# The second block one chunk behind the first, its mixing ahead of the first group means, and the adapter's weights later

## What is computed

```
L0 cond:  y = einsum('bct,bcd->bdt', x, w[subject])           # mixes the 64 tokens of a sample
L0 ffn:   gu = y @ Wq_gu^T ; h = silu(gate) * up ; hn = rms_norm(h) ; x = x + hn @ Wq_p^T
          Wq = ternary quantisation of W in groups of 64 (scale = mean |w| of the group)
L1 cond:  H = x @ W^T + (x @ A[idx]^T) @ B[idx]^T * s[idx]    # a low-rank adapter per sample
L1 ffn:   router logits, softmax over 8 experts, the best 2, weighted sum of expert outputs ; x = x + that
```

## Time and profile before

| | |
|---|---|
| runs, median (lowest to highest) | 2326.0 us (2324.54 to 2328.16) |
| the profiled execution | 2326.22 us |
| its span in the trace | 2324.5 us |
| TensorE busy | 2296.1 us, 99% |
| VectorE busy | 1669.5 us, 72% |
| ScalarE busy | 1146.7 us, 49% |
| mean granted clock of TensorE | 0.998 |

### The profile page before, as it was taken

One profiled execution on the slowest core, in us unless ns is written; L12 is line 12 of the kernel. 1 busy time (PEld: TensorE's weight loads), 2 busy tenths in 40 slices (PEclk: granted clock), 3 DMA queues, 4 the chain that ended last, 5 costly groups with the idle time before them and its releaser, 6 DMA issues.

```text
span 2324.5 us, 30032 instructions
## 1 busy us (share of the span) xinstructions
PE 2296.1 (99%) x10288; PEld 1893.4 (81%) x10288; DVE 1669.5 (72%) x2497; ACT 1146.7 (49%) x1685; POOL 11.2 (0%) x20
## 2 busy tenths in 40 slices
PE   7999999999999998999999999999999999999999
PEld 5777888888888887888888888888888888888887
DVE  8985434334343435888899999998988888888883
ACT  7754333333232324788888888888522222222221
POOL 0000000000000000000000000000000000000000
PEclk9999999999999999999999999999999999999999
DMA  5314202111111115121111112114422222222220
GB/s 200 109 41 138 75 19 74 37 56 56 54 38 54 72 36 199 59 82 62 56 68 68 68 59 81 54 63 162 173 91 72 90 93 70 89 94 70 89 81 23
DMA packets 103332, 184.66 MB, mean 79 GB/s; under 512 B 12210, under 2 KB 45554, under 8 KB 100978
## 3 DMA queue, kind: packets, MB, share of 16 engines
q1 hardware_dynamic: 51554, 124.77, 15.3%
q10 hardware_dynamic: 51600, 59.25, 7.7%
q0 software_dynamic: 128, 0.07, 0.0%
HBM read 122.72 MB, written 61.34 MB: 79 GB/s over the span
## 4 chain that ended last, share of the span: by engine, by line
PE 91%; issue 5%; DVE 2%; ACT 1%; DMA 1%; ACTq 0%; POOLq 0%; POOL 0%; SPq 0%; DVEq 0%
PE slot L1501 17%; PE ex L1672 10%; PE ex L1673 10%; PE ex L1674 10%; PE plane L1633 10%; PE plane L1635 10%; PE plane L1637 10%; PE pj L1514 8%; PE slot L1554 3%; PE slot L1476 1%; PE slot L1543 1%; PE slot L1533 1%; DVE ew_lo L1386 0%; PE slot L1486 0%; DMA q_raw<-in_w_ffn 0%
## 5 line engine op out<-in xcount | busy, mean ns | idle before, releaser
L1501 PE MATMUL slot<-y_hi,wgu 128*128 128x512 f32 x1024 | 403.1, 394 | 2.2 <-DVE q_scale L1052 1.7
L1501 PE MATMUL slot<-y_lo,wgu 128*128 128x512 f32 x1024 | 399.1, 390 | 0.0
L1633 PE MATMUL plane<-rw_hi,hb 128*128 128x512 f32 x1008 | 393.3, 390 | 1.7 <-ACT plane L855 0.9
L1635 PE MATMUL plane<-rw_hi,hb 128*128 128x512 f32 x1008 | 393.1, 390 | 0.0
L1637 PE MATMUL plane<-rw_lo,hb 128*128 128x512 f32 x1008 | 392.9, 390 | 0.0
L1672 PE MATMUL ex<-ew_hi,hb 128*128 128x512 f32 x992 | 386.0, 389 | 0.2 <-ACT ex L983 0.2
L1673 PE MATMUL ex<-ew_hi,hb 128*128 128x512 f32 x992 | 385.9, 389 | 0.0
L1674 PE MATMUL ex<-ew_lo,hb 128*128 128x512 f32 x992 | 385.9, 389 | 0.0
L983 ACT ACTIVATE ex<-eb_sb 128x512 f32<-128x512 f32 x248 | 149.0, 602 | 449.2 <-DVE acc L1415 386.1
L1361 DVE SCALAR_TENSOR_TENSOR lead_in<-code_in,wts 128x1024 bf16<-128x1024 bf16 x256 | 311.4, 1216 | 1.2
L1094 DVE TENSOR_TENSOR hid<-gate,slot 128x512 f32<-128x512 f32 x112 | 76.9, 687 | 221.7 <-ACT gate L690 221.1
(11 more groups left out here) (155 smaller groups left out, 3222.2 us busy)
## 6 DMA issues: line engine op xcount, KB each, us to landing
hb<-h_scratch SPq DMA_DIRECT2D x34, 512.0 KB, 3.3
h_scratch<-ht ACTq DMA_DIRECT2D x64, 256.0 KB, 3.1
code_scratch<-half_code SPq DMA_DIRECT2D x64, 256.0 KB, 2.0
half_in<-code_scratch SPq DMA_DIRECT2D x32, 512.0 KB, 3.3
hb<-h_scratch ACTq DMA_DIRECT2D x30, 512.0 KB, 3.6
q_raw<-in_w_ffn SPq DMA_DIRECT2D x21, 512.0 KB, 3.4
x_scratch<-x_res ACTq DMA_DIRECT2D x8, 1024.0 KB, 4.5
rraw<-in_rwT SPq DMA_DIRECT2D x8, 1024.0 KB, 10.9
```

The costliest lines, as they stand in the source:

```text
L1501: last = mm(slot[s % 2][:, g, :], wgu[:, c, r * P:(r + 1) * P], y[:, c, :], start=(c == 0 and v == 0), stop=(c == DC - 1 and v == 1))
L1633: mm(bank[:, :, :], hb[:, u, c, 0, :], rw_hi[:, w, c, o], start=False, stop=False, skip_group_check=True)
L1635: mm(bank[:, :, :], hb[:, u, c, 1, :], rw_hi[:, w, c, o], start=False, stop=False, skip_group_check=True)
```

## The change

Block 1 runs one chunk behind block 0 and not two (`AHEAD = 1`): pair h issues block 1's chunks 2h-1 and 2h, and only chunk 15 is left for after the loop. Block 1's mixing goes from behind gu(0,1) to directly behind gu(0,0), ahead of the two group means of that pair, on TensorE, ScalarE and VectorE. AT, Bt, the indices and the scalings are loaded behind `load_raw(8)` into buffers of their own (which share their place with the lo parts); `small_weights` goes from the end of the pair h = 0 to just ahead of `linear_weights`, on ScalarE and VectorE, and the product's wait for it is gone. Behind the loop, chunk 1's `second_hidden` comes ahead of the last silu and product of block 1. On TensorE the adapter product and the two linear products of block 0 each go one down product later.

```diff
-AHEAD = 2
+AHEAD = 1
...
     FIRST.append(f"gu{_j}@0")
     GU_ORDER.append((0, _j))
     if _h:
-        FIRST.append(f"gu{_j - 2}@1")
-        GU_ORDER.append((1, _j - 2))
-    FIRST += [f"q{k}" for k in quant_of(_h)[:2]]
-    FIRST.append(f"gu{_j + 1}@0")
-    GU_ORDER.append((0, _j + 1))
-    if _h:
         FIRST.append(f"gu{_j - 1}@1")
         GU_ORDER.append((1, _j - 1))
     else:
         FIRST += ["mix0@1", "mix1@1"]
+    FIRST += [f"q{k}" for k in quant_of(_h)[:2]]
+    FIRST.append(f"gu{_j + 1}@0")
+    GU_ORDER.append((0, _j + 1))
+    FIRST.append(f"gu{_j}@1")
+    GU_ORDER.append((1, _j))
     FIRST += [f"q{k}" for k in quant_of(_h)[2:]]
...
+        small_raw = ExitStack()
+        a_raw = sb("a_raw", [P, DC, P], F32, small_raw)
+        b_raw = sb("b_raw", [P, D], F32, small_raw)
+        small_raw.close()
         a_lo = sb("a_lo", [P, DC, P], F32R, pa)
+        b_lo = sb("b_lo", [P, D], F32R, pa)
         b_hi = sb("b_hi", [P, D], F32R, pa)
-        b_lo = sb("b_lo", [P, D], F32R, pa)
...
             gather_mix(1, mixw1, mixw1_in, range(3, SPB))
-            sp.dma_start(hid1[:, RING - 2, :].rearrange("p (c n) -> p c n", c=DC),
-                         AT.rearrange("(c p) n -> p c n", p=P)).then_inc(raw_small, 16)
-            sp.dma_start(hid1[:, RING - 1, :], Bt).then_inc(raw_small, 16)
-            sp.dma_start(idx_i[:, :], idx6).then_inc(small_in, 16)
-            sp.dma_start(scal_sb[:, :], scal).then_inc(small_in, 16)
             for k in range(5, NU):
                 load_raw(k)
+                if k == 8:
+                    sp.dma_start(a_raw[:, :, :], AT.rearrange("(c p) n -> p c n", p=P)).then_inc(raw_small, 16)
+                    sp.dma_start(b_raw[:, :], Bt).then_inc(raw_small, 16)
+                    sp.dma_start(idx_i[:, :], idx6).then_inc(small_in, 16)
+                    sp.dma_start(scal_sb[:, :], scal).then_inc(small_in, 16)
...
@@ ScalarE
                 silu(0, j)
                 quant_out(3 * h + 1)
                 if h:
-                    silu(1, j - 2)
+                    silu(1, j - 1)
+                else:
+                    mix(1)
                 quant_out(3 * h + 2)
...
                 high(0, j + 1, hid[:, (j + 1) % 2, :])
-                if h:
-                    silu(1, j - 1)
-                else:
-                    mix(1)
+                silu(1, j)
                 if h < PAIRS - 2:
                     quant_in(3 * h + 6)
-                if h == 0:
-                    small_weights()
             second_hidden(0)
-            silu(1, HC - 2)
-            for p in range(1, 4):
+            second_hidden(1)
+            silu(1, HC - 1)
+            for p in range(2, 4):
                 second_hidden(p)
-            silu(1, HC - 1)
             store_x1(0)
+            small_weights()
             linear_weights()
...
@@ VectorE
                 n, s = use(1, f"gu{j}")
                 dve.wait_ge(gate_ready, gu_count(1, j) + 1)
-                if j in (RING - 2, RING - 1):
-                    dve.wait_ge(w_lo_ready, 2)
...
                 product(0, j)
                 if h:
                     squares(0, j - 1)
-                    second_product(j - 2)
+                    second_product(j - 1)
+                else:
+                    mix(1)
...
                 low(0, j + 1, hid[:, (j + 1) % 2, :])
-                if h:
-                    second_product(j - 1)
-                else:
-                    mix(1)
+                second_product(j)
                 if more:
                     quant_sign(b)
-                if h == 0:
-                    small_weights()
             squares(0, HC - 1)
             finish(0)
             second_hidden(0)
-            second_product(HC - 2)
-            for p in range(1, 4):
+            second_hidden(1)
+            second_product(HC - 1)
+            for p in range(2, 4):
                 second_hidden(p)
-            second_product(HC - 1)
+            small_weights()
             linear_weights()
...
@@ TensorE
                 gu(0, j)
                 if h:
-                    gu(1, j - 2)
+                    gu(1, j - 1)
+                else:
+                    mix(1)
                 if more:
                     quant(3 * h + 3)
...
                 gu(0, j + 1)
-                if h:
-                    gu(1, j - 1)
-                else:
-                    mix(1)
+                gu(1, j)
                 proj(0, j)
...
-                if p == 4:
+                if p == 5:
                     adapt(0)
-                if p == 6:
+                if p == 7:
                     linear(0, 0)
-                if p == 9:
+                if p == 10:
                     linear(0, 1)
```

More of the change, by code:

```diff
@@ L156, in first_block @@
     return isinstance(i, int) and i == 0
-assert len(REST) % 2 == 0 and len(FIRST) % 2 == 0 and len(SECOND) % 2 == 0
+assert len(REST) % 2 == 0 and (len(FIRST) + len(SECOND)) % 2 == 0
 def build(nc, x, idx7, idx6, cond_w, w_ffn, WcT, AT, Bt, scal, rwT, rb, ewT, eb, out):
@@ L638, in small_weights @@
                 act.wait_ge(raw_small, 32)
-                nc.scalar.activation(a_hi[:, :, :], hid1[:, RING - 2, :].rearrange("p (c n) -> p c n", c=DC), ACT.Copy).then_inc(w_hi_ready, 1)
-                nc.scalar.activation(b_hi[:, :], hid1[:, RING - 1, :], ACT.Copy).then_inc(w_hi_ready, 1)
+                nc.scalar.activation(a_hi[:, :, :], a_raw[:, :, :], ACT.Copy).then_inc(w_hi_ready, 1)
+                nc.scalar.activation(b_hi[:, :], b_raw[:, :], ACT.Copy).then_inc(w_hi_ready, 1)
             def linear_weights():
@@ L1020, in small_weights @@
                 dve.wait_ge(w_hi_ready, 2)
-                nc.vector.tensor_tensor(a_lo[:, :, :], hid1[:, RING - 2, :].rearrange("p (c n) -> p c n", c=DC),
+                nc.vector.tensor_tensor(a_lo[:, :, :], a_raw[:, :, :],
                                         a_hi[:, :, :].bitcast(F32), ALU.subtract).then_inc(w_lo_ready, 1)
-                nc.vector.tensor_tensor(b_lo[:, :], hid1[:, RING - 1, :], b_hi[:, :].bitcast(F32), ALU.subtract).then_inc(w_lo_ready, 1)
+                nc.vector.tensor_tensor(b_lo[:, :], b_raw[:, :], b_hi[:, :].bitcast(F32), ALU.subtract).then_inc(w_lo_ready, 1)
                 dve.wait_ge(small_in, 32)
```

## The result

The changed kernel took 2328.46 us (median of 18 runs, 2327.57 to 2332.85), the kernel before 2324.59 us in the same session (18 runs, 2324.03 to 2328.45). The ratio is 1.0018, 95% interval 1.0011 to 1.0024: slower by about 4 us. The interval leaves out no change, and the difference is just under the 0.2% that the prediction called a difference. The profiled execution of the changed kernel has a span of 2329.0 us against 2324.5.

What follows compares the result with a forecast made beforehand. TensorE bounds the kernel, busy 2296.1 of 2324.5 us; only its idle can be won. 2326.22 - 2.4 + 2.5 + 0.9 = 2327.2, against the median 2326.0: 2327.0 us, range 2325 to 2330.

Steps and rivals of the forecast that it cites:

- Part 1: First pair, 23 to 50 us: TensorE reaches quant(7) 1.3 us later with 3.64 us more done, -2.4 us.
- part of the 2.4: First pair: small weights' removal takes 1.91 us off VectorE, counted within the 2.4 us gain, not separately.
- Part 2: Pairs 1 to 7: same step order and drains, cost 0; bounds 0 and 0.3 us for each pair.
- Rival C: Steady pairs no longer close, TensorE waits for quant(a)'s scale: 2 to 5 us more, 2329 to 2332; chance 0.10.
- Part 3: End of the opening, from row sums' end to adapter product: idle 4.4 us in place of 1.95, +2.5 us.
- the forecast's idle of 4.4: TensorE's idle between row sums' end and adapter product: 20.7 us less 16.3 us of work.
- only 0.65 of VectorE's 1.91 lasts: Small weights ahead of the linear weights: 1.25 of VectorE's 1.91 us goes into existing waits, 0.65 delays.
- Rival B: End doesn't bite: adapter product's input ready 20.07 us or less behind row sums' end; 2324 us, chance 0.21.
- Part 4: Behind the second linear product: only four down products follow, the last waits for its split, +0.9 us.
- T at about 175.1: Sign of being right: the row-sum matmuls end at about 175.1 us, against 177.46 before.
- rival E: TensorE falls to its low clock after longer idle; adapter product and two down products cost 5 us: 2332, chance 0.05.

Runs made afterwards that it cites:

- mix_early: Kernel before with only block 1's mixing moved directly behind gu(0,0), still two chunks apart, small weights where they were: median 2329.89 us.
- small_late: Kernel before with only the small weights in own buffers, loaded behind load 8 and split ahead of the linear weights: median 2324.04 us, ratio 0.9994.
- fill_end: Changed kernel with eight idle matmuls ahead of block 0's adapter product: median 2328.97 us.
- small_pair7: Changed kernel with small_weights moved to the end of pair 7 on ScalarE and VectorE: median 2327.42 us.
- fill_front: Changed kernel with eight idle matmuls in the first pair, six between quant(3) and quant(4), two behind quant(4): median 2328.59 us.
- after: The changed kernel itself, as first measured and profiled against the kernel before: median 2328.46 us, ratio 1.0018.
- after_again: The changed kernel measured once more, nothing edited: median 2330.26 us.
- lin_back: Changed kernel with block 0's second linear product back behind position 9 of the down products: median 2329.74 us.
- best: Kernel before plus small weights in own buffers, loaded late and split where engines are idle, and the adapter product behind down product 5: median 2320.95 us, ratio 0.9977.
- before_adapt5: Kernel before with only block 0's adapter product behind down product 5, not 4: mean 2324.3 us, ratio 0.9994.

## Why the prediction was right or wrong

It gave 2327.0 us and +1.0 us; measured were 2328.46 and +3.9 us. The time lies in the range and within 0.2%, where 0.84 of the chance stood. That it is only 1.5 us off is in part luck: the forecast started from a median of three, 2326.0, and the median of 18 is 1.4 us lower, so as a change it is 2.9 us off. The direction was right and the schedule nearly (+1.5 for +1.0). Of the rest of the miss, low clock in the opening, to which the sum gave nothing, is about 1.4 us in the means, and what is left is open. Part of the 3.9 is that the median of the kernel before falls among its executions at 0.999 and that of the changed kernel among those at 0.998. Of the executions at 0.998 the changed kernel's take 2328.1 us and those of the kernel before 2326.3: 1.8 apart, close to the schedule's 1.5.

**Part 1, the first pair: mechanism right, size off by 0.4.** The waits stand where it put them: quant(3) 0.38, quant(4) 1.62, gu(0,1) 0.52 us (forecast 0.35, 1.6, 0.7), and gu(1,0) runs directly behind. (One of quant(3)'s two matmuls is absent from that trace; where both are there, in `mix_early`, the wait is 0.16.) The forecast counts a little differently: from the release to gu(0,1) it has 5.31 us, and it is 5.55; the pair of products behind takes 7.55 at full clock and not 7.40. Without low clock release to T is 154.07 to 154.09, 1.65 longer than before with 3.64 more work: -2.0 us, not -2.4. With it, 1.65 us more are lost. The runs of single parts show what this net is made of, if the parts simply add up: the early mixing costs 2.16, the small weights' removal gives 1.89, and the rest, the second block one chunk behind, gives 1.65 - 2.16 + 1.89 = 1.38 longer with 3.64 us more done, so 2.3 us; it covers the down product's wait of 2.0 that the mixing opens. That the removal of the small weights was "part of the 2.4" was an understatement: it is nearly all of it.

**Part 2, the steady pairs: right.** From 50 to 170 us TensorE is busy 119.59 us in the changed kernel (120.00 before), and the list of waits names none there. The 0.41 are six group means of which the trace has one matmul only, starting 0.07 us after the step ahead of it ends; the step itself is no longer than the others. Rival C is out.

**Part 3: right in the sum, the reading of it too kind.** The adapter product came at T+20.71; forecast T+20.7. The first down product waits 1.0 us (forecast 1.1) and the adapter product 1.9; a second wait of 0.7 us, of down product 4 behind the small and the linear weights on VectorE, is in the forecast's idle of 4.4 but was not named. That only 0.65 of VectorE's 1.91 lasts held in the changed kernel (+0.64), but alone on the kernel before the same move costs 1.14. Rival B is out.

**Part 4: right.** 0.7 us of wait and a slower restart ahead of down product 14; undoing the move gave 1.0 us, forecast 0.9.

**The sum without low clock** is +1.5 between the same points (+1.54, +1.46 and +1.44 in three traces), against the forecast's +1.0; the missing half is part 1.

**A slip.** "T at about 175.1" contradicts the prediction's own sum: quant(7) 1.3 us later and no change in the steady pairs puts T at 178.8. Measured without low clock it is 178.63 from a release at 24.54, or 179.1 for the release at 25.04. A reader who had used that line to test the steps would have found a fault that isn't one.

**The clock, rival E, is where the forecast failed.** It put the clock at nothing in its sum and at 0.05 as a rival, by two waits ahead of the first products (4.33 us low, 2.15 us not). Neither carries that. The first pair of the same trace takes just as long:

```profile
5.42 1.01 PE L1486 MATMUL slot<-q_mag,group_mean 128*128 128x512 bf16 x2 [5.42 <-ACT q_mag L660]
```

So the pair behind 4.33 us of idle was no slower than the one before it, and a fall of the clock in between isn't shown. And behind the 2.15 us the clock was low in two other traces. What happened is a fall of the clock where several short waits stand near each other: 0.38, 1.62 and 0.52 us with a group mean between them, and 1.0, 0.7 and 1.9 us within 17 us, with down products between. No wait of these is as long as 2.15, and a single one of 2.9 in `small_late` was followed by no fall. So the length of the last wait doesn't decide it. Nor do short waits near each other by themselves: the same three in the first pair kept the clock at 1.00 in the traces of `fill_end` and `small_pair7`, and the same three at the adapter product did in `fill_front`. The price was too high: the low clock lasts about 3.4 us, not the adapter product and two down products, and costs 1.65 and 1.55 us, 3.2 together, not 5. Weighted with 13 of 29 executions this is 1.4 us of the mean, if 0.996 stands for both stretches. The Trainium skill (TensorE: Matmul & The Clock Gate, HAM oscillation) says that idle gaps between groups of matmuls can bring the clock down. The traces of the changed kernel agree, at 0.50 in both stretches. The next section of the same page of the Trainium skill (A second HAM failure mode: psum-queue depth-cycling) tells of a clock that swings because the engine idles briefly and often between groups of matmuls. That is nearer to this case than the long wait I weighed; when it happens it doesn't say, and some traces here kept their clock with the same waits.

**What stays open.** The means of the changed kernel and of the one before differ by about 3.8 us; 1.5 of schedule and 1.4 of low clock in the opening leave 0.9. A candidate is the end of block 7, where TensorE is idle for 4.1 us in both kernels and a stretch of low clock follows, or begins in it, whose length varies. Windows of the kernel before, and then of the kernel with late small weights:

```profile
900.00:905.00 5.00, 2.56 (x12) 0.66 1.00 415
905.00:910.00 5.00, 4.23 (x13) 0.50 1.01 412
910.00:915.00 5.00, 5.00 (x19) 0.81 1.02 420
```

```profile
900.00:905.00 5.00, 3.28 (x16) 0.69 1.04 417
905.00:910.00 5.00, 4.10 (x19) 0.97 1.00 403
910.00:915.00 5.00, 5.00 (x23) 1.00 1.03 426
```

Low clock there adds up to (0.34 + 0.50 + 0.19) x 5 / 0.5 = 10.3 us in the first and 3.4 us in the second. Each 3.4 us of it costs up to 1.7 us, less where it lies over idle; the 0.999 and the 0.998 group of the kernel before are 1.6 apart. The changed kernel was never in the 0.999 group in 29 runs; two traces of it show 10.3 us there. The moment of the release is another candidate, since it moves an execution by itself and was seen only in traces. Whether an opening of another length makes that stretch longer was not tried. Why one execution has the two stretches in the opening and another has not is open as well. The three traces with both (`after`, `after_again`, `lin_back`) have their release at 25.02 to 25.30 us, and those of the same first pair without (`fill_end`, `small_pair7`) at 26.00; so the moment at which the waits fall may matter, but five traces don't show it. Nor is it settled why `small_pair7`, with the changed kernel's first pair, had no execution at 0.996, and so whether the fillings or something that moves with any edit took the upper peak away; the 0 of 33 against 13 of 29 fits the first and doesn't prove it.

## What to carry to other kernels

Where TensorE is the bound and an order is written by hand, list its waits and ask for each what short work is ready at that moment: one down product ahead of the adapter product closed a wait of 1.8 us and gave 1.8, and 1.9 us of VectorE work taken from under a wait gave 1.9. Its new place took 1.1 of that back; in `best`, at another place and with the adapter product later, nothing was taken back. A step that moves into a gap brings its own hand-overs; the mixing was 3.6 us of work for a 1.5 us gap, and what waits for its splits cost more than the gap. Waits too short to worry about one by one can go with a fall of the clock: add its price (here 1.6 us a time) to the slower end of the range, don't take one wait that kept the clock as proof that the next will, and read several executions by their mean granted clock before giving a difference of a few microseconds a cause.

## What the runs showed of the hardware

The granted clock fell to 0.50 behind waits none of which was longer than 1.94 us, within 1 us after work had resumed and for about 3.4 us. Two traces of the changed kernel show it, and by their mean clock 13 of its 29 executions had it. The same idle of 2.15 us ahead of a group mean left the clock at 1.00 in twelve traces and had it at 0.50 in two; 2.9 us ahead of the adapter product left it at 1.00. In the first 20 us the windows give a granted clock of 1.00, while matmuls run slowly: the pair of group-mean matmuls takes 1.03 us against 0.59 later, and the first mixing took 4.8 to 6.1 us in the traces against 3.73 for the same 32 matmuls in block 2. The pair took the same 1.01 us where the windows do give 0.50, in `before_adapt5`. So a low clock that the windows don't give is the likely reading of this stretch, from the durations only. And the changed kernel's adapter product ran slowly beside heavy DMA traffic (share 0.96), but at full speed beside the same traffic (0.94) in the execution with the filled wait: the clock did it, not the transfers.
